# Cross-attention worked by pairs of chunks instead of single chunks, in a gated attention and FFN block

## The reference, cut to what matters

```python
q = split_heads(xn @ Wq) * DH ** -0.5            # xn: layer norm of x
k, v = split(context @ Wkv)                      # 16 heads of 64
k = concat(null_kv[0], k)                        # 129 keys
v = concat(null_kv[1], v)
attn = softmax(q @ k.T, axis=-1)
out = (attn @ v) @ Wout
out = layer_norm(out) * ln_scale + ln_bias
x = x + tanh(g_xattn) * out                      # called x2 here
x = x + tanh(g_ffn) * ffn(layer_norm(x))         # quantised, gated FFN
```

## Time and profile before

| what | value |
| --- | --- |
| median of three runs | 581.29 us (580.51 to 581.66) |
| the profiled execution, its own time | 581.69 us |
| its span, first to last instruction | 579.6 us |
| TensorE busy | 529.9 us, 91% |
| VectorE busy | 408.3 us, 70% |
| ScalarE busy | 311.9 us, 54% |
| GpSimd busy | 123.5 us, 21% |
| DMA moved | 25.86 MB, mean 45 GB/s |

### The profile page before, as it was taken

One profiled execution on the slowest core, in us unless ns is written; L12 is line 12 of the kernel. 1 busy time (PEld: TensorE's weight loads), 2 busy tenths in 40 slices (PEclk: granted clock), 3 DMA queues, 4 the chain that ended last, 5 costly groups with the idle time before them and its releaser, 6 DMA issues. The chain is left out here.

```text
span 579.6 us, 10953 instructions
## 1 busy us (share of the span) xinstructions
PE 529.9 (91%) x3936; PEld 458.1 (79%) x3936; DVE 408.3 (70%) x1051; ACT 311.9 (54%) x878; POOL 123.5 (21%) x129
## 2 busy tenths in 40 slices
PE   2999999999999999999999999998779999807898
PEld 2877889888888988898898888887467878604797
DVE  4679844855674675476458457848686888999996
ACT  2734633543444263354336326525668659988992
POOL 3001310230130132023113102312303118930000
PEclk9999999999999999999999999999999999957899
DMA  7932001100110110020011001002201000000033
GB/s 255 357 116 74 1 1 54 40 2 1 54 36 0 54 36 0 0 90 0 0 54 36 0 1 38 1 2 93 73 18 33 5 2 0 6 32 0 2 95 124
DMA packets 18478, 25.86 MB, mean 45 GB/s; under 512 B 1216, under 2 KB 15808, under 8 KB 18448
## 3 DMA queue, kind: packets, MB, share of 16 engines
q1 hardware_dynamic: 18192, 25.17, 13.2%
q0 software_dynamic: 256, 0.30, 0.3%
HBM read 21.27 MB, written 4.19 MB: 44 GB/s over the span
## 5 line engine op out<-in xcount | busy, mean ns | idle before, releaser
L843 ACT ACTIVATE probs<-bank,nmax 128x129 f32<-128x129 f32 x256 | 90.9, 368 | 123.0 <-DVE nmax L1205 123.0
L1637 POOL TENSOR_TENSOR probs<-probs,rinv 128x512 f32<-128x512 f32 x64 | 66.7, 1043 | 333.2 <-DVE rinv L1213 333.2
L615 PE MATMUL bank<-wv,ctxT 128*128 128x512 f32 x384 | 94.5, 398 | 0.0
L607 PE MATMUL bank<-ctxT,wk 128*128 128x256 f32 x672 | 88.9, 282 | 0.1
L607 PEld LDWEIGHTS bank<-ctxT,wk 128*128 128x128 f32 x672 | 83.6, 188 | 0.3 <-DVE ctxT L1072 0.3
L615 PEld LDWEIGHTS bank<-wv,ctxT 128*128 128x128 f32 x384 | 70.4, 188 | 16.9 <-issue 1.2
L851 ACT ACTIVATE oT<-bank,ncol 128x256 fp32r<-128x256 f32 x64 | 30.6, 478 | 52.9 <-PE bank L679 52.8
L1217 DVE COPY pT<-bank 128x512 f32<-128x512 f32 x64 | 43.5, 680 | 18.0 <-PE bank L669 17.6
L607 PE MATMUL bank<-xnT,wq 128*128 128x256 f32 x336 | 54.7, 298 | 1.0 <-DVE v L1132 1.0
L843 ACT ACTIVATION_READ_ACCUMULATOR probs<-bank,nmax 128x1 f32 x256 | 51.9, 203 | 0.0
L607 PEld LDWEIGHTS bank<-xnT,wq 128*128 128x128 f32 x336 | 43.1, 188 | 8.3 <-issue 1.2
(11 more groups left out here) (170 smaller groups left out, 831.3 us busy)
## 6 DMA issues: line engine op xcount, KB each, us to landing
craw<-in_ctx SPq DMA_DIRECT2D x8, 512.0 KB, 3.5
stage<-in_L_xattn_Wkv SPq DMA_DIRECT2D x8, 512.0 KB, 12.1
xa<-in_x SPq DMA_DIRECT2D x8, 256.0 KB, 2.8
xr<-in_x SPq DMA_DIRECT2D x8, 256.0 KB, 2.9
x_scratch<-y SPq DMA_DIRECT2D x7, 256.0 KB, 2.2
x2all<-x_scratch SPq DMA_DIRECT2D x1, 1792.0 KB, 8.5
xres<-x_scratch SPq DMA_DIRECT2D x6, 256.0 KB, 2.9
out<-yout SPq DMA_DIRECT2D x6, 256.0 KB, 2.2
```

The costliest lines, as they stand in the source:

```text
L607: last = mm(bk[:, n * TG:(n + 1) * TG], wt[a][:, k, f], act_t[b][:, k, :], start=(k == 0 and i == 0), stop=(k == kk - 1 and i == len(TERMS ...
L615: last = mm(bk[:, :], ctxT[a][:, k, b * S:(b + 1) * S], wv[w][:, k, h * 512:(h + 1) * 512], start=(k == 0 and i == 0), stop=(k == KC - 1 a ...
L843: last = nc.scalar.activation(probs[:, c % 2, u, 0:NK], score_bank[c % 2][h][:, b * QW:b * QW + NK], ACT.Exp, bias=nmax[:, c % 2, u:u + 1] ...
L1637: G.tensor_tensor(probs[:, c % 2, :, 0:S], probs[:, c % 2, :, 0:S], rinv[:, c % 2, :].rearrange("p (u o) -> p u o", o=1).to_broadcast([P, ...
```

## The change

The step of the attention becomes a pair of chunks (`NP = 4` pairs to a group). In step `p` TensorE does the scores of pair `p+1` (8 matmuls into two banks, 128 columns each), the units named `ahead`, the transposes of pair `p` (8, in two halves `h`), the values of pair `p-1` (8 matmuls, one whole bank) and the units named `behind`. The null key no longer rides in the scores: it is subtracted from all keys when they are read out of PSUM (`keys`, so a `Q` unit is read by two instructions), the maxima are clamped at zero by a further small instruction, and the null key's own exponential is one small instruction to a half (`null_exp`), added to the sum ahead of the reciprocal. VectorE's chains for the norm of the group before stand together in step 1, those of the input in step 2, `x2_statistics` and `x2_range` in the tail. `W` waits for the last two pairs one after the other instead of for all ahead of its first matmul. `Q6` moves from the penultimate to the final group. SyncE reads x2 back in two loads, of which the first stands ahead of the final group's own transfers.

The tables and the functions of the steps:

```diff
-    PLAN = ([["Q0"], ["Q1"], ["Q2"], ["Q3"], ["Q4"], ["Q5", "V00"], ["Q6", "V10"], ["Q7", "X"]],
+    PLAN = ([(["Q0", "Q1"], ["Q2"]), (["Q3", "Q4", "Q5"], []), (["Q6", "Q7"], []), (["V00", "V10", "X"], [])], [],
             ["V01", "V11", "C", "W"])
...
+    PLAN_PENULT = ([(["Q0"], ["Q1"]), (["Q2", "Q3"], []), (["Q4", "Q5"], []), (["V00", "V10"], [])], [], ["W"])
+    PLAN_FINAL = ([(["Q6"], ["Q7"]), ([], ["V01"]), (["V11"], []), (["F0", "F1"], [])], ["F2", "F3", "F4"],
+                  ["F5", "F6", "F7", "F8", "W"])
...
-                        if b == 0:
-                            wait(pe, ot_lo, g * NS + NS)
                         for k in range(KF):
+                            if b == 0 and k % 2 == 0 and k >= KF - 4:
+                                pe.wait_ge(ot_lo, g * NP + k // 2 + 1)
...
+            def scores(g, p):
+
+                if isinstance(g, int) and g == NG - 1 and p == NP - 1:
+                    unit_read(g, FINAL.index("Q7"))
+
+                wait(pe, pt_copied, 2 * (g * NP + p) - 3)
+                for u in range(4):
+                    c, b = 2 * p + u // GB, u % GB
                     for h in range(2):
                         rows = slice(h * DH, (h + 1) * DH)
+                        last = mm(score_bank[p % 2][h][:, u * S:(u + 1) * S], qk[rows, c, b, :],
+                                  qk[rows, c, GB + b, :], start=True, stop=True)
...
+            def prob_transposes(g, p, h):
+                n = 2 * (g * NP + p) + h
+                pe.wait_ge(norm_done, n + 1)
+                if h == 1:
+                    wait(pe, pt_copied, n - 1)
+                pt = transposed(p, h)
...
+            def values(g, p):
+                wait(pe, pt_copied, 2 * (g * NP + p) + 2)
+                if 0 < p < NP - 1:
+                    pe.wait_ge(ot_lo, g * NP + p)
...
+                for p in range(NP):
+                    if p + 1 < NP:
+                        scores(g, p + 1)
+                    ahead, behind = slots[p]
+                    run(ahead)
+                    for h in range(2):
+                        prob_transposes(g, p, h)
+                    if p:
+                        values(g, p - 1)
+                    run(behind)
+                if not (isinstance(g, int) and g == NG - 1):
                     scores(g + 1, 0)
+                run(mid)
+                values(g, NP - 1)
+                run(tail)
```

ScalarE, VectorE, GpSimd and SyncE:

```diff
+            def exps(g, p, h):
+                act.wait_ge(max_done, 2 * (g * NP + p) + h + 1)
+                wait(act, pt_done, 2 * (g * NP + p) - 2)
                 for u in range(4):
+                    nc.scalar.activation(probs[:, p % 2, h, u, :], score_bank[p % 2][h][:, u * S:(u + 1) * S], ACT.Exp,
+                                         bias=nmax[:, p % 2, h, u:u + 1], accum_out=rowsum[:, p % 2, h, u:u + 1])
+
+                nc.scalar.activation(null_exp[:, p % 2, h, :], nmax[:, p % 2, h, :], ACT.Exp).then_inc(exp_done, 1)
...
                 if not final:
+                    exps(g + 1, 0, 0)
+                run(mid)
+                out_high(g, NP - 1)
+                if not final:
+                    exps(g + 1, 0, 1)
+                run(tail)
...
+            def maxima(g, p, h):
+                n = 2 * (g * NP + p) + h + 1
+                if h == 0:
+                    dve.wait_ge(scores_done, g * NP + p + 1)
+                V.tensor_reduce(nmax[:, p % 2, h, :], score_bank[p % 2][h][:, :].rearrange("p (u s) -> p u s", s=S),
+                                AX.X, ALU.max, negate=True).then_inc(keys_max, 1)
+                dve.wait_ge(keys_max, n)
+
+                V.tensor_scalar(nmax[:, p % 2, h, :], nmax[:, p % 2, h, :], 0.0, None, ALU.min).then_inc(max_done, 1)
...
+                def beside(p):
+
+                    if p == (0 if final else 1) and not first:
+                        attention_rstd(g - 1)
+                        attention_norm(g - 1, y)
+                    if p == 2 and feeds(g):
+                        ln_stats(g + 2)
+                        ln_rstd()
+                        ln_apply()
...
+                for p in range(NP):
+                    ahead, behind = slots[p]
+                    if p + 1 < NP:
+                        for h in range(2):
+                            maxima(g, p + 1, h)
+                    if not final:
+                        beside(p)
+                    run(ahead)
+                    for h in range(2):
+                        prob_copy(g, p, h)
+                    if p + 1 < NP:
+                        for h in range(2):
+                            inverse_sums(g, p + 1, h)
+                    if p:
+                        out_low(g, p - 1)
+                    if final:
+                        beside(p)
+                    run(behind)
...
+                        if u == "F8":
+                            x2_statistics(g - 1, y[:, :, :])
...
+            def normalise(g, p, h):
+                pool.wait_ge(rinv_done, 2 * (g * NP + p) + h + 1)
...
+            sp.wait_ge(unit_done, units(NG - 1)[1] + FINAL.index("Q7") + 1)
+            all_back(0, NG - 2, x2all_in)
             group_dma(NG - 1)
...
+            all_back(NG - 2, NG - 1, x2all_late)
```

More of the change, by code:

```diff
@@ L651, in unit @@
                 last.then_inc(unit_done, 1)
-            def scores(g, c):
-                if isinstance(g, int) and g == NG - 1 and f"Q{c}" in FINAL:
-                    unit_read(g, FINAL.index(f"Q{c}"))
-                wait(pe, exp_done, g * NS + c - 1)
-                for b in range(GB):
+            def scores(g, p):
[4 more added lines that the diff above has]
+                    c, b = 2 * p + u // GB, u % GB
@@ L668, in prob_transposes @@
                 for u in range(4):
-                    last = nc.tensor.transpose(pt_bank[:, u * P:(u + 1) * P], probs[:, c % 2, u, 0:S], ident[:, :])
+                    last = nc.tensor.transpose(pt[:, u * P:(u + 1) * P], probs[:, p % 2, h, u, :], ident[:, :])
                 last.then_inc(pt_done, 1)
-            def values(g, c):
-                wait(pe, pt_copied, g * NS + c + 1)
-                if 0 < c < NS - 1:
-                    pe.wait_ge(ot_lo, g * NS + c)
-                for b in range(GB):
+            def values(g, p):
+                wait(pe, pt_copied, 2 * (g * NP + p) + 2)
+                if 0 < p < NP - 1:
+                    pe.wait_ge(ot_lo, g * NP + p)
+                if isinstance(g, int) and g == NG - 1 and p == NP // 2:
+                    unit_read(g, FINAL.index("V11"))
+                for u in range(4):
+                    c, b = 2 * p + u // GB, u % GB
@@ L677, in values @@
                     for h in range(2):
                         rows = slice(h * DH, (h + 1) * DH)
-                        last = mm(value_bank(c)[rows, b * S:(b + 1) * S], v[:, b, c, rows],
-                                  pT[:, c % 2, 2 * h + b, :], start=True, stop=True)
+                        last = mm(value_bank(p)[rows, u * S:(u + 1) * S], v[:, b, c, rows], pT[:, p % 2, h, u, :],
+                                  start=True, stop=True)
                 last.then_inc(pv_done, 1)
@@ L1152, in attention_stats @@
                     last = V.bn_stats(bn[:, 2 + b, :], bk[:, b * D:(b + 1) * D])
-                ln2.count(last)
-                maxima(g + 1, 1)
-                ln2.wait()
+                ln2.link(last)
                 settle()
@@ L1367, in group, with run @@
+                first, penult = peeled and g == 0, peeled and g == NG - 2
+                pos, (slots, mid, tail) = 0, plan(g)
+                def run(part):
+                    nonlocal pos
+                    for u in part:
+                        if u == "C":
+                            ctx_low(g + 2)
+                            continue
                         split(g, pos)
                         pos += 1
-                    if c < NS - 1 and weights:
-                        inverse_sums(g, c + 1)
@@ new lines, in group @@
+                if not final:
+                    for h in range(2):
+                        maxima(g + 1, 0, h)
+                run(mid)
+                out_low(g, NP - 1)
+                if not final:
+                    inverse_sums(g + 1, 0, 0)
+                run(tail[:1])
+                if not final:
+                    inverse_sums(g + 1, 0, 1)
+                run(tail[1:])
+                if first:
+                    weight_values(1)
+                    weight_scales(2)
+                elif not final:
+                    x2_statistics(g - 1, y[:, :, :])
+                    x2_range(g - 1, y[:, :, :])
@@ L1650, in group @@
                                         ALU.add).then_inc(xgb_ready, 1)
-                    normalise(g, c)
-                if not (isinstance(g, int) and g == NG - 1):
-                    normalise(g + 1, 0)
+                    for h in range(2):
+                        if p + 1 < NP:
+                            normalise(g, p + 1, h)
```

(2 more changed lines are left out.)

272 lines of the change are left out of this document (107 added, 165 removed).

## The result

The changed kernel takes 567.36 us (median of 4 runs, 565.77 to 568.44), the kernel before on the same chip 580.90 (580.26 to 581.66): ratio 0.9761, 95% interval 0.9743 to 0.9779. The forecast was 567.0 us with a range of 562.0 to 573.5. The profiled execution took 565.77 us, the fastest of the four, with a span of 564.0 us against 579.6 before, 15.6 us less.

The account below looks back on a forecast made before the run. TensorE's own sequence, with time lost to shape changes, bounds the loop; the final group waits for probabilities. -15.4 - 0.3 - 0.3 + 2.0 + 1.2 - 2.8 + 1.1 = -14.5 us gave 567.0 us, range 562 to 573.5.

Parts of the forecast that it names:

- The packs: Groups 0 to 6: packs of eight pay shape changes once per two chunks, 0.55 us a pair, -15.4 us in all.
- Narrower scores: Score matmuls of 128 columns instead of 130: 0 to -0.6 us, taken as -0.3.
- Loop waits: TensorE stays covered in the loop: 0, bounds 0 and 1.3 us a group; the edge is step 3's copies.
- rival 4: Loop, step 1: VectorE becomes the bound, each of seven groups loses 2.5 us, 584.7 us; chance 0.04.
- Prologue: Before the first Q unit: later sums delay layer norm and V00's split on VectorE, +2.0 us, bounds 0 and +3.
- Group 0: First group: -2.6 us, including -0.3 from idle mostly due to FFN weights on VectorE ahead of a reciprocal.
- W of group 6: W directly follows the last values and stops inside for the last pair's outputs: +1.2 us, bounds 0 and +2.
- Group 7: Final group: -0.6 us; blocks from 31.3 to 30.7 us with Q6 gained, waits about 8 again, 38.8 us.
- Rival 1: Waits less than counted: prologue and W cost nothing, group 7 gives 2 us more, about 562 us; chance 0.14.
- Rival 2: Cover in the loop's step 3 breaks, both copies exposed in seven groups: 576 us, or 571 with half; chance 0.16.
- rival 5: Packs of eight run no faster because weight loads set the pace: first term 0, 582 us; chance 0.03.
- Rival 3: Group 7: longer waits bring TensorE's clock to 1.2 GHz, slowing W, F units and transposes: 575 us; chance 0.05.

Follow-up runs that it names:

- run 1: Changed kernel with transposes and values interleaved in halves (four transposes, four values of the pair before, twice): 573.43 us.
- run 2: Changed kernel with a pair's scores in two packs of four and the first Q unit between them, groups 0 to 6: 578.23 us.
- run 3: Kernel before with score blocks of 128 columns instead of 130, null key left out, null value kept: 581.09 us, ratio 0.9991.
- run 6: Changed kernel with x2_range of the group before (two reductions) moved to step 3, ahead of the last pair's copies, groups 1 to 6: 572.74 us.
- Run 12: Changed kernel with the moves of run 4 and run 7, but pair 0's sums and reciprocals later, behind V01's split: 563.62 us.
- run 5: Changed kernel with pair 0's sums and reciprocals of group 0 moved behind V10's split on VectorE in the prologue: 567.09 us.
- run 7: Changed kernel with run 5's move, and the FFN weights' scales moved from the prologue to group 0's first step: 566.54 us.
- run 4: Changed kernel with V10 of group 6 moved from step 3 to the tail, ahead of W: 566.33 us.
- run 9: Changed kernel with the edits of run 4, run 5, run 7 and run 8 together: 564.15 us.
- run 8: Changed kernel, final group's VectorE order altered: pair 3's maxima earlier, sums directly behind each half's copy, V11's split behind both: 566.67 us.

## Why the prediction was right

The mechanism was right: fewer changes of shape on a TensorE that nothing else holds up, less a few exposed waits. That the median came within 0.4 us of the forecast is in part luck. By the traces the pieces give 15.6 us and not 14.5, and the medians 13.5.

**The packs** (-15.4 over seven groups). Pitch, price of a change of shape and count all held: 2.2 us a group, 2.21 measured. Runs 1 and 2 give 4.8 and 6.3 us of the loop's 11.0 back by cutting the packs again with the same matmuls. Their prices, 0.32 and 0.42 a place, add to more than 0.55, because a cut made alone opens boundaries that the cycle of the earlier trace rows doesn't have: transposes behind values (0.59 instead of 0.53, run 1) and a Q unit's twelve matmuls in front of scores (1.51 instead of 1.43, run 2).

**Narrower scores** (-0.3). Not told from nothing by the times of run 3; its five loop groups are 0.33 us shorter.

**Loop waits** (0). Right, by 0.36 us in step 3 (run 6). In step 1 VectorE was idle for 2.37 us before the copies, so rival 4 was far.

**Prologue** (+2.0, measured +1.78). The chain was the one followed: sums behind the second half's exponentials, then the layer norm, V00 and V11. Run 12, with the moves of runs 5 and 7 as well, took 2.6 us of distance away, by moving VectorE's work and leaving none out.

**Group 0** (-2.6, measured -3.14). A term was left out here. Before, seven chunks' scores stand between the first Q unit and the next group; now it is three pairs, so six. One chunk's scores, 0.65 us, moved ahead of the first Q unit, where TensorE waits anyway. The idle of 0.39 us fell to 0.10, as counted.

**W of group 6** (+1.2). The stop is 0.93 us, and run 4, which covers it, shortens group 6 by 1.17.

**Group 7** (-0.6, measured -0.81). Close by luck, since errors cancel. The prediction's blocks were too short on both sides: TensorE was busy 33.16 us before and not 31.3, and 33.06 after and not 30.7. The nine F units take about 5.2 us in the changed kernel and not 9 x 0.45, and the transposes of `probs` 4.3 and not 3.9. Its waits were too long on both sides: 6.3 us before and not 8.2, and 38.66 - 33.06 = 5.6 after and not 8. The stop of 1.3 at pair 1 was 0.3 (its transposes take 1.35 us instead of 1.04), pair 3's was 2.1 instead of 3, and those among F4 to F8 and W 3.1 instead of 4. So shorter waits gave 0.7 us and shorter blocks 0.1, where the prediction had nearly all in the blocks.

**Behind group 7** (+1.1, measured +1.05). `x2_statistics` moved as counted.

**The rivals.** Rival 1 fell: the waits of the prologue and of W came nearly in full, and group 7 gave 0.2 us more, not 2. Rival 2 missed by the 0.36 us of run 6. Rivals 4 and 5 fell with the loop groups at 47.33 us. Rival 3 did not come in the profiled execution of the changed kernel, where group 7 stands at 1.00. In four of the eleven runs on the changed kernel it did come there, and in run 3 too, which has the waits of the kernel before, at 1.3 to 1.5 us and not 8 (last section). So the fall is commoner than 0.05 suggests, it needs no longer waits, and its price was put too high.

## What to carry to other kernels

A TensorE that is busy all the time may still lose a sixth of the time of its small packs (0.55 of 3.54 us a pair here) to changes of shape: compare the pitch of the same matmuls in a long row with their pitch in a short pack, multiply by the packs, and merge. Before merging, find the one step where the helper engines' last result is due, and measure its room, since here two reductions of 0.6 us put there cost 0.81 us a group. When work is moved on VectorE, look at what it releases on GpSimd, and what VectorE does at that moment. Where a change is worth about 1 us, compare the pieces of the traces, since a late start or a fall of the clock moves a whole execution by as much.

## What the runs showed of the hardware that was not expected

**VectorE and GpSimd.** The apply of 0.73 us took 2.14 us and ended at 45.03, just behind GpSimd's products at 44.88 (run 5). In the changed kernel's group 7 a step of the root on 128x2 values, 0.17 us elsewhere, ends with the product that began as it did. VectorE's row and GpSimd's:

```profile
378.47 1.05 DVE L1130 TENSOR_SCALAR rs<-rs 128x2 int32<-128x2 int32 x1
...
378.46 1.04 POOL L1705 TENSOR_TENSOR probs<-probs,rinv 128x512 f32<-128x512 f32 x1 [0.46 <-DVE rinv L1267]
```

The Trainium skill (SBUF — State Buffer, SBUF: two separate sides) states that the two share a pair of ports, which a GpSimd instruction, or a VectorE instruction of certain kinds, holds to its end, and that the other then blocks fully. The rows agree: the end of the late instruction follows the product's end, not its own length. The prediction had no such term. In the loop it did not matter, as TensorE never waits there. In group 7 the late step stands in the chain ahead of pair 2's maxima and of the copies for which TensorE waits 0.33 us at 384.54, so it may have cost some of that; no run tests it.

**The clock.** In the profiled execution of run 9, W of group 7 took 7.31 us at a granted clock of 0.77. In run 8 the same W took 5.80 us at 1.00. The stretch ahead of it has TensorE busy for 3.98 us in both. Busy time by stretch, run 9 and then run 8:

```profile
396.23:402.14 5.91, 3.98 (x36) 2.94 (x36) 3.91 (x7) 3.61 (x7) 0.00 (x0) 1.00 0.01 3
402.14:409.45 7.31, 7.30 (x48) 7.31 (x49) 6.12 (x28) 4.35 (x10) 0.00 (x0) 0.77 0.00 0
```

```profile
399.92:405.84 5.92, 3.98 (x36) 2.94 (x36) 3.92 (x7) 3.61 (x7) 0.00 (x0) 1.00 0.01 3
405.84:411.64 5.80, 5.80 (x49) 5.80 (x49) 5.19 (x24) 3.16 (x8) 0.00 (x0) 1.00 0.00 0
```

A mean of 0.77 lies between the two levels, 1.2 and 2.4 GHz: part of W ran at the lower. Run 9 was not the only one. The clock also fell in group 7 of the profiled executions of runs 2, 6 and 7, at pair 3's transposes and values, and of run 3, a relative of the kernel before, in W. Run 7, and then the same work in the changed kernel:

```profile
392.70:399.27 6.57, 4.74 (x32) 3.60 (x33) 4.61 (x9) 2.36 (x5) 1.04 (x1) 0.74 0.00 0
```

```profile
393.00:398.26 5.26, 3.36 (x32) 2.55 (x32) 4.63 (x10) 2.36 (x5) 1.04 (x2) 1.00 0.00 0
```

In the 7.00 us ahead of these stretches TensorE was busy 5.59 us in run 7 and 5.61 in the changed kernel. Group 7 took 40.0 us in runs 2, 6 and 7 instead of 38.7, and the stretch behind it was as long as ever (153.8 to 154.0 us), so there the fall cost 1.3 us in full. In run 9 W took 1.5 us longer, but the stretch behind group 7 was 1.0 us shorter than in run 8 (152.85 against 153.86), so 0.5 was left. In run 8 the clock fell in the prologue, to 0.77 from 20 to 25 us, and the first maximum stood latest there, at 37.18. So rival 3's place was the right one, and such a fall costs up to 1.5 us here and not the 8 of the prediction. What makes it come in one execution and not in another stays open; only one execution of each kernel was profiled.
